# Where a row shift of a layer norm is computed: one VectorE operation in three stages, two ScalarE operations in a fourth

## The reference, cut to what matters

```python
x = x + _layernorm(_L0_attn_ref(_layernorm(x), Wq, Wk, Wv, Wo))
x = x + _layernorm(_L0_ffn_ref(_layernorm(x), w_gate, w_up, w_down))
x = x + _layernorm(_L1_attn_ref(_layernorm(x), ...))      # latent attention
x = x + _layernorm(_L1_ffn_ref(_layernorm(x), ...))

def _layernorm(x, eps=1e-05):
    return (x - mean(x)) / sqrt(var(x) + eps)
```

## Time and profile before

| | |
|---|---|
| median of the runs | 3118.07 us |
| the profiled execution, its time | 3119.57 us |
| its span | 3117.8 us |
| TensorE, VectorE, ScalarE, GpSimd busy | 92%, 60%, 41%, 34% |
| stage l0o, first to last operation | about 630 to 710 us |
| stage w | about 1278 to 1373 us |
| stage l1p of batch 1 | about 2035 to 2129 us |
| stage f1n | about 2686 to 2731 us |

### The profile page before, as it was taken

How to read it: one execution, slowest core, us unless ns; L and a number is a source line. 1 busy time by engine, 2 the same in 40 slices (tenths; PEclk the granted TensorE clock), 3 DMA queues, 4 the chain that set the end, 5 groups by cost and what they waited for, 6 DMA issues and landing times. The chain is left out here.

```text
span 3117.8 us, 43250 instructions
## 1 busy us (share of the span) xinstructions
PE 2859.3 (92%) x14636; PEld 2285.1 (73%) x14636; DVE 1877.8 (60%) x3698; ACT 1289.4 (41%) x2488; POOL 1053.2 (34%) x842
## 2 busy tenths in 40 slices
PE   7969999878999999688999999777999999599998
PEld 5846666557888888467888888666888888478886
DVE  5647888674544545635666666665666666744446
ACT  2216666653222222433444444333444444543335
POOL 1217877754645546414111111042111110132223
PEclk9979999988999999789999999899999999799999
DMA  4774444141121101570000000121000000200012
GB/s 163 235 225 133 128 131 128 54 149 63 53 80 49 62 25 36 183 271 16 13 18 12 12 18 3 77 81 35 12 18 12 12 12 4 101 21 21 10 37 81
DMA packets 136084, 217.87 MB, mean 70 GB/s; under 512 B 14512, under 2 KB 85168, under 8 KB 135440
## 3 DMA queue, kind: packets, MB, share of 16 engines
q1 hardware_dynamic: 135952, 216.19, 21.7%
HBM read 144.05 MB, written 71.83 MB: 69 GB/s over the span
## 5 line engine op out<-in xcount | busy, mean ns | idle before, releaser
L1525 ACT ACTIVATE l1a_probs<-l1a_scores,l1a_row 128x128 f32<-128x128 f32 (+7 forms) x256 | 189.4, 741 | 319.9 <-DVE l1a_row L1572 319.9
L1259 POOL TENSOR_TENSOR l0a_probs_hl<-l0a_probs,l0a_probs_hl 128x896 fp32r<-128x896 f32 (+1 forms) x128 | 284.9, 2245 | 107.4 <-ACT l0a_probs L1187 107.4
L1582 DVE TENSOR_TENSOR l1a_pT_hl<-l1a_work,l1a_pT_hl 128x512 fp32r<-128x512 f32 (+3 forms) x384 | 213.1, 555 | 170.1 <-ACT l1a_pT_hl L1532 169.9
L1499 PE MATMUL l1a_obank<-l1a_pT_hl,l1k_v_hl 128*128 128x512 f32 (+3 forms) x1152 | 300.3, 370 | 7.1 <-DVE l1a_pT_hl L1582 7.1
L1634 POOL TENSOR_TENSOR l1k_wabs<-l1a_wabs_raw,l1k_wabs 128x384 fp32r<-128x384 f32 x28 | 28.4, 1015 | 801.7 <-ACT l1k_wabs L1541 801.7
L1479 PE MATMUL l1a_scores<-l1k_kT_hl,l1a_qa_hl 128*128 128x512 f32 (+3 forms) x1152 | 290.8, 361 | 1.5 <-ACT l1a_probs L1525 1.5
L1507 PE MATMUL l1a_work<-l1a_wov,l1a_oT_hl 128*128 128x512 f32 x768 | 215.1, 403 | 5.0 <-DVE l1a_oT_hl L1601 3.0
L1532 ACT CAST l1a_pT_hl<-l1a_work 128x512 fp32r<-128x512 f32 (+3 forms) x384 | 183.5, 478 | 82.8 <-PE l1a_work L1490 81.5
L1572 DVE TENSOR_REDUCE l1a_row<-l1a_scores 128x1 f32<-128x128 f32 (+7 forms) x256 | 189.8, 751 | 44.0 <-PE l1a_scores L1482 43.9
L1596 DVE SCALAR_TENSOR_TENSOR l_acc<-l1a_work,l1a_row,l_acc 128x512 f32<-128x512 f32 x256 | 189.0, 748 | 27.1 <-PE l1a_work L1507 20.3
L1499 PEld LDWEIGHTS l1a_obank<-l1a_pT_hl,l1k_v_hl 128*128 128x128 f32 x1152 | 180.9, 191 | 33.3 <-DVE l1a_pT_hl L1582 14.8
(11 more groups left out here) (283 smaller groups left out, 6416.3 us busy)
## 6 DMA issues: line engine op xcount, KB each, us to landing
v_dram<-l0f_v_rows SPq DMA_DIRECT2D x24, 768.0 KB, 4.0
qk_dram<-l0f_stage SPq DMA_DIRECT2D x128, 128.0 KB, 2.5
l0a_v_stage<-v_dram SPq DMA_DIRECT2D x32, 384.0 KB, 4.5
l0a_q_stack<-qk_dram SPq DMA_DIRECT2D x32, 256.0 KB, 3.5
l0a_k_stack<-qk_dram SPq DMA_DIRECT2D x32, 256.0 KB, 4.0
f0f_chunk<-in_L_ffn_w_gate_up SPq DMA_DIRECT2D x32, 256.0 KB, 2.6
l1a_wov_raw<-wov_dram SPq DMA_DIRECT2D x32, 256.0 KB, 2.7
l0a_v_stage<-v_dram SPq DMA_DIRECT2D x8, 768.0 KB, 6.4
```

The costliest lines, as they stand in the source:

```text
L1259: nc.gpsimd.tensor_tensor(probs_hl[:, r, 1, 0:wide], probs[:, r, 0:wide], f32(probs_hl[:, r, 0, 0:wide]), ALU.subtract).then_inc(low_done, 1)
L1499: last = pe.matmul(obank[:, c:SPAN], src["v_hl"][:, a, n, :], pT_hl[:, ring(n, s), b, c:SPAN], start=(n == 0 and i == 0), stop=(n == QT * ...
L1525: nc.scalar.activation(probs[s][:, first:first + wide, :].rearrange("p k c -> p (k c)"), scores[:, n % S_AHEAD, 0:wide * P], ACT.Exp, bias ...
L1582: nc.vector.tensor_tensor(pT_hl[:, r, 1, c:SPAN], work[:, slot, c:SPAN], f32(pT_hl[:, r, 0, c:SPAN]), ALU.subtract).then_inc(work_free[slo ...
```

## The change

In the three norm stages `inverse` loses `minus`. `shift` is made by one `scalar_tensor_tensor` on VectorE, (mean * -1.0) * rstd, behind `rstd`. The tiles `minus` and `zero`, their semaphores, the memset of `zero` and the wait for it go too.

In `latent_operands` VectorE keeps only `r_inv` of the three. ScalarE makes `r_minus` (ACT.Copy of the mean with the constant scale -1.0) right behind `r_std`, for row tile i - 1, and `r_shift` (ACT.Copy of `r_minus` with the column `r_inv` as scale) right ahead of the scaled row tile, for row tile i - 2.

```diff
             def inverse(which, t):            # the same in l0o, w and f1n
                 r = t % RING
-                dve.wait_ge(mv_done[which], t + 1)
-                nc.vector.tensor_tensor(minus[:, which, r:r + 1], zero[:, :], mv[:, which, r, 0:1], ALU.subtract
-                                        ).then_inc(minus_done[which], 1)
                 dve.wait_ge(std_done[which], t + 1)
                 nc.vector.reciprocal(rstd[:, which, r:r + 1], std[:, which, r:r + 1]).then_inc(rstd_done[which], 1)
-                dve.wait_ge(minus_done[which], t + 1)
                 dve.wait_ge(rstd_done[which], t + 1)
-                nc.vector.tensor_tensor(shift[:, which, r:r + 1], minus[:, which, r:r + 1], rstd[:, which, r:r + 1],
-                                        ALU.mult).then_inc(shift_done[which], 1)
+                nc.vector.scalar_tensor_tensor(out=shift[:, which, r:r + 1], in0=mv[:, which, r, 0:1], scalar=-1.0,
+                                               in1=rstd[:, which, r:r + 1], op0=ALU.mult, op1=ALU.mult
+                                               ).then_inc(shift_done[which], 1)
...
                     act.wait_ge(r_mv_done, t + 1)           # latent_operands, ScalarE
                     nc.scalar.activation(r_std[:, t % 2:t % 2 + 1], r_mv[:, t % 3, 1:2], ACT.Sqrt, bias=eps_ln[:, 0:1]
                                          ).then_inc(r_std_done, 1)
+                    wait(act, r_shift_done, t - 1)
+                    nc.scalar.activation(r_minus[:, t % 2:t % 2 + 1], r_mv[:, t % 3, 0:1], ACT.Copy, scale=-1.0
+                                         ).then_inc(r_minus_done, 1)
                 if rows is not None and i >= 2:
                     t = i - 2
+                    act.wait_ge(r_minus_done, t + 1)
+                    act.wait_ge(r_inv_done, t + 1)
+                    wait(act, r_z_done, t - 1)
+                    nc.scalar.activation(r_shift[:, t % 2:t % 2 + 1], r_minus[:, t % 2:t % 2 + 1], ACT.Copy,
+                                         scale=r_inv[:, t % 2:t % 2 + 1]).then_inc(r_shift_done, 1)
                     act.wait_ge(r_shift_done, t + 1)
...
-                    dve.wait_ge(r_mv_done, t + 1)           # latent_operands, VectorE
-                    nc.vector.tensor_tensor(r_minus[:, t % 2:t % 2 + 1], zero[:, :], r_mv[:, t % 3, 0:1], ALU.subtract
-                                            ).then_inc(r_minus_done, 1)
                     dve.wait_ge(r_std_done, t + 1)
                     wait(dve, r_z_done, t - 1)
                     nc.vector.reciprocal(r_inv[:, t % 2:t % 2 + 1], r_std[:, t % 2:t % 2 + 1]).then_inc(r_inv_done, 1)
-                    dve.wait_ge(r_minus_done, t + 1)
-                    dve.wait_ge(r_inv_done, t + 1)
-                    nc.vector.tensor_tensor(r_shift[:, t % 2:t % 2 + 1], r_minus[:, t % 2:t % 2 + 1],
-                                            r_inv[:, t % 2:t % 2 + 1], ALU.mult).then_inc(r_shift_done, 1)
```

More of the change, by code:

```diff
@@ L183, in residual_norm_transposed @@
     stats, mv = m.sb("stats", [P, 2, RING, 6]), m.sb("mv", [P, 2, RING, 2])
-    std, rstd, minus, shift = (m.sb(n, [P, 2, RING]) for n in ("std", "rstd", "minus", "shift"))
-    zero = m.sb("zero", [P, 1])
+    std, rstd, shift = (m.sb(n, [P, 2, RING]) for n in ("std", "rstd", "shift"))
     eps = m.sb("eps", [P, 1])
@@ L191, in residual_norm_transposed @@
     next_loaded, stored = m.sem("next_loaded"), m.sem("stored")
-    stats_done, mv_done, minus_done, std_done, rstd_done, shift_done = ([m.sem(f"{n}{i}") for i in range(2)] for n in (
-        "stats_done", "mv_done", "minus_done", "std_done", "rstd_done", "shift_done"))
-    zero_set = m.sem("zero_set")
+    stats_done, mv_done, std_done, rstd_done, shift_done = ([m.sem(f"{n}{i}") for i in range(2)] for n in (
+        "stats_done", "mv_done", "std_done", "rstd_done", "shift_done"))
     eps_set, z_done, sum_done, normed, turned, high_done, low_done = (m.sem(n) for n in (
```

18 lines of the change are left out of this document (3 added, 15 removed).

## The result

The changed kernel takes 3098.49 us (median of 4 runs, 3093.06 to 3101.19), the kernel before 3119.2 beside it (4 runs, 3117.04 to 3122.82). The ratio is 0.993, with a 95% interval from 0.9912 to 0.9949: faster, by more than the 0.2% that the forecast took as the least that can be told. The forecast was 3102.5 with a range from 3096 to 3112. Three executions among the experiments took far longer than all others (3604.09, 7095.32 and 9672.37 us) and count in no ratio.

What follows compares the result with a forecast made beforehand. TensorE was busy 92% of the span, but VectorE operations with two SBUF tiles waiting for GpSimd set the pace in some stages. Savings 8.6 + 4.0 + 1.5 + 1.5 = 15.6 took 3118.07 to 3102.5 us, range 3096 to 3112.

Steps and rivals of the forecast that it cites:

- l1p: Stage l1p (`latent_operands`): steps fall from 10.29 us as the stall leaves the chain; -8.6 us, between -6.5 and -10.5.
- the sum: l1p: start distances along the step's chain add to 8.59 us, with 0.15 and 0.30 for the two new ScalarE operations.
- f1n: Stage f1n, VectorE back to back: 24 x 0.06 and one stalled `minus`; -1.5 us, between -1 and -2.
- the path through `k_parts`: l1p: the step's chain runs through `k_parts`; in two steps it stands 0.4 us behind GpSimd, making them about 9.0.
- l0o: Stage l0o: `minus` stalls go, partly passing to `shift`; -4.0 us, between -1.5 and -6.7.
- the middle, 0.55: l0o's steady steps: each saves between 0.37 and 1.06 us, taken as 0.55 for 5 steps, 2.75 in all.
- The tail: End of l0o: three stalled `minus` at 0.33 and free ones at 0.06, counted as 1.3 us saved.
- w: Stage w: five stalls and some ten free `minus` make 2.2 us; 1.5 passed on, between 0 and 3.
- (a): Rival: the stall only moves to `k_parts`, `normed` or `shift`; l1p gives 2, norm stages 3; 3113 us, chance 0.14.
- (b): Rival: `shift` slips ahead of GpSimd each time in l0o and w, l1p's clock stays up; 3096 us, chance 0.16.
- (c): Rival: Copy forces two table loads in each l1p step, making the kernel slower; 3126 us, chance 0.03.
- (d): Rival: a lower-clock stretch shifts onto heavy products, 2.4 us a batch, ten batches needed; slower, 3126 us, chance 0.04.

Runs made afterwards that it cites:

- experiment 3: The changed kernel, but in l1p `r_shift` is one `scalar_tensor_tensor` on VectorE, nothing on ScalarE: 3100.25 us, ratio 0.9944 against the kernel before.
- Experiment 4: The changed kernel, but everywhere, l1p included, `shift` is one VectorE `tensor_scalar` with `rstd` as column operand: 3085.9 us, ratio 0.9897 against the kernel before.
- 5: The kernel before, but in l0o `minus` is a `tensor_scalar` reading one tile, operation count kept: 3111.05 us, ratio 0.9973; l0o 72.4 us.
- 9: The kernel before, but in l0o `shift` takes `rstd` as a column operand, `minus` kept: 3111.76 us, ratio 0.9981; l0o 75.9 us.
- 6: The kernel before with l0o alone changed, plus an unused 128x384 VectorE memset ahead of each tile's first `shift`: 3106.98 us, ratio 0.9965; l0o 72.4 us.
- experiment 11: The kernel before with l0o alone changed, plus an unused 128x1024 VectorE memset ahead of each tile's first `shift`: 3110.12 us, ratio 0.9973; l0o 74.8 us.
- 7: The kernel before with l0o alone changed, plus an unused 128x384 VectorE memset behind each tile's first `shift`: 3106.56 us, ratio 0.9962; l0o 70.2 us.
- experiment 8: The kernel before with the change in stages w and f1n alone: 3113.31 us, ratio 0.9983.
- 10: The kernel before, but in l1p `r_minus` is a VectorE `tensor_scalar` reading one tile, `r_shift` kept: 3114.68 us, ratio 0.9989; l1p 90.3 us.

## Why the prediction was right or wrong

**What was right.** The direction, and that a VectorE operation with two SBUF tiles waits for GpSimd, the new one too: experiment 3 and the means of 551, 420 and 355 ns. l1p: -8.4 against -8.6, in part by luck (below), with steps of 8.62, 8.63, 8.86, 8.58 and 8.61 us where 8.59 and two of 9.0 were forecast. The two Copies start 0.10 us apart and the scaled tile comes 0.41 behind the first, where the sum had 0.45; the estimate from the Trainium skill (ScalarE: Activation LUTs, What ACT_TABLE_LOAD costs), 0.19 and 0.28, is what the rows show (188 and 283 ns). Between them the details offset each other: from the first `r_stats` to the last it went 9.1 us faster (the two unstalled steps paid 0.26 together, as forecast), and two batches of products at the lower clock, 7.10 and 5.77 us, took 12.87 where the kernel before had 6.75 and 4.34. The clock did not give anything back. A further 1.05 us lie ahead of the first `r_stats`, where no norm runs yet: that part took 9.50 us in the profile before and 8.45 in the one after, but 8.3 to 8.6 in five of the other seven profiles with the old code. Without this accident of the pair l1p would have given about 7.3. f1n: -1.3 in this pair, between -1.3 and -2.4 over the profiles, forecast -1.5.

**What was wrong in l1p: the path through `k_parts`.** The prediction let the chain of a step run through `k_parts` and had a stall of 0.4 us there lengthen two steps to 9.0. The steps took 8.86 and 8.58; from 10.92 and 10.93 they gained 2.06 and 2.35 instead of 1.90. VectorE's next operation, `inv`, waits for ScalarE's `root`, which comes from `down` and not from `k_parts`. The first row is of the kernel before, the second of the changed one, in a step in which `k_parts` was held:

```profile
2075.06 0.17 DVE L2585 RECIPROCAL l1p_inv<-l1p_root 128x2 f32<-128x2 f32 x1 [1.17 <-ACT l1p_root L2550]
```

```profile
2074.47 0.17 DVE L2569 RECIPROCAL l1p_inv<-l1p_root 128x2 f32<-128x2 f32 x1 [0.70 <-ACT l1p_root L2536]
```

VectorE stood idle for 1.17 us between `k_parts` and `inv`, and a stall of 0.5 only took from that. (In the step of 8.86 another 0.3 us passed between `inv` and `normed`; the rows give no reason.) Experiment 4 agrees: `k_parts` took 0.95 and 0.94 us in two steps, 0.7 of it stall, and both steps stayed under 8.4. The sum of 8.59 was not hurt, for `down` and `k_parts` keep their distance in all other steps; but a stall of 0.7 us at `k_parts`, the longest seen, costs a step nothing.

**What was wrong: the size of l0o.** The term was -4.0, between -1.5 and -6.7; the stage lost 11.9, of which 10.4 repeat at an equal clock. Three pieces of the working failed, each by its own words.

"ScalarE's work releases GpSimd and moves as well, so I take the middle, 0.55, for the 5 steps." (The middle of its own bounds, 0.37 and 1.06, is 0.72, so 0.55 was below it; at 0.72 the five steps would have come to 3.6.) The steps fell to TensorE's pace, the upper end that I had worked out: 5.0 us against 2.75. Two places of contention in one tile, 1.0 and 0.5 us long, held VectorE to a cycle of 4.26; either of them freed (5 and 9) brings all or most tiles down to the next bound. That much is shown. The rest is read from the rows: I had treated the stage as a chain in which a stall moves on. It is a cycle with another bound 1 us below, and as soon as VectorE's own step is under that bound (3.01 and 2.77 in the later tiles of the changed kernel, with one `shift` held), the stall that remains costs nothing. The slip of the other `shift` ahead of GpSimd is seen in just these tiles; where both are held VectorE needs 3.65 to 3.75, and TensorE got over that for three tiles by running further ahead. So the slip, a margin of 0.10 us, may well carry part of the gain; experiments 6 and 11 were to decide it and could not.

"Before them TensorE's products set the pace": 1.05 us came from there. The likely reason, argued and not tested, is that VectorE's stalls begin there too: three `minus` and four `shift` are held in that part of the kernel before.

"The tail has three stalled `minus` and seven free ones: 1.3." It lost 4.3. (3 x 0.33 and seven free ones at 0.06 would be 1.4; the sum took five.) The norms of the last tiles are behind the products by what the steps before have piled up. TensorE's first waits for `xn` in the tail were 2.08 and 3.90 us; now two tiles' transposes run together at 685.21, and the waits are 2.37 and 1.38. A tail is priced with the backlog that the steady part leaves to it, not with its own operations alone. That reading is argued from the rows; what stands behind it is that the tail goes with the steps over most of the table (31.1 with 21.4, 27.9 with 20.1, 27.8 with 19.4, 26.2 with 17.8, 26.1 with 17.1). It is not the whole: at 25.8 and 25.9 the tail runs from 15.8 (4, no stall left) over 17.5 (7) to 18.1 (6), so its own operations count as well.

**w** stays open. -3.2 in this pair, -1.5 forecast, and a scatter of 4 us with the same code. The two halves (experiment 8) give -2.2 to -8.1 for w and f1n together, which holds the forecast of -3.0.

**The rivals.** (a), the stall that only moves, is a real mechanism and decides where the next operation with two tiles follows directly: experiments 3 and 10 are this rival, at 9.95 us a step. In the changed kernel the next one in l1p was `k_parts`, 0.3 us behind GpSimd's end, as the prediction had it. (b), more than forecast, came true for l0o alone. Its clock part did not. The 3098.49 us measured lie at the very edge between the bracket given to the forecast (3098.5 to 3108) and this rival. (c): no table load stands between the operations of l1p. (d): the two slow batches of l1p cost 1.8 us more than before, far from ten.

The total of 15.6 was too small by 5 to 6 us (20.7 by the medians, 21.8 by the ratio), and the one term of l0o is enough to account for that: 6.4 us too small at an equal clock.

## What to carry to other kernels

When small VectorE operations show durations of 0.4 to 1.8 us, look for a GpSimd operation that ends with them and count the tiles that they read. Give the second one as a per-row column operand, and the stall is gone: experiment 4 won 32 us where moving or merging the operations won 21. When a stage runs in a cycle, compare the cycle with the next bound below it: in l0o a stall removed took it down to that bound, with the tail behind it, even while other stalls of the same kind remained on view.

## What the runs showed that I had not expected

A `shift` that followed directly on a memset was not held by GpSimd's addition although it began up to 0.96 us into it (experiment 11: 0.10 us at 674.96, with GpSimd from 674.22 to 675.52), as long as the memset had begun no later than 0.13 us behind GpSimd. With two short operations between memset and `shift` it was held: in experiment 7 a memset began at 654.85, 0.09 us behind GpSimd, and the `shift` at 655.34 took 0.72. The Trainium skill (SBUF — State Buffer, Who interferes with whom) gives the shared interfaces to whichever starts first, for the whole instruction, and on this chip doesn't count a memset among the holders; this row doesn't fit that, and what lies behind it was not tried.

The clock of 0.92 in the first part of l0o comes and goes between profiles of kernels with the same l0o, and moves that part by 1.3 to 1.6 us.
